# Two mixtures of five paths on VectorE and GpSimd, without identity products on TensorE

## What is computed

```
probs = softmax(logits / tau[:, None], -1)
eps = sigmoid(eps_logit) * 0.2
probs = probs * (1.0 - sum(eps, -1, keepdims=True)) + eps
o = einsum('blhp,blhpd->blhd', probs, paths)          # P = 5 paths
o = o * rsqrt(mean(o * o, -1, keepdims=True) + 1e-05) * norm_w
return o.reshape(b, Ln, D) @ Wo
```

## Time and profile before

| | us |
|---|---|
| median of 3 runs | 425.94 |
| lowest, highest | 425.29, 427.28 |
| the profiled execution | 425.43 |
| its span, first to last instruction | 423.6 |
| TensorE busy (share of the span) | 359.7 (85%) |
| VectorE busy | 308.6 (73%) |
| ScalarE busy | 274.8 (65%) |
| GpSimd busy | 42.0 (10%) |

### The profile page before, as it was taken

One profiled execution on the slowest core, in us unless ns is written; L12 is line 12 of the kernel. 1 busy time (PEld: TensorE's weight loads), 2 busy tenths in 40 slices (PEclk: granted clock), 3 DMA queues, 4 the chain that ended last, 5 costly groups with the idle time before them and its releaser, 6 DMA issues.

```text
span 423.6 us, 9739 instructions
## 1 busy us (share of the span) xinstructions
PE 359.7 (85%) x4096; PEld 267.9 (63%) x4096; DVE 308.6 (73%) x487; ACT 274.8 (65%) x431; POOL 42.0 (10%) x103
## 2 busy tenths in 40 slices
PE   5599999999999898899588379566599994969996
PEld 3387786677866675798576365433267763558885
DVE  2896578737649988999576967867858899597433
ACT  4789875879779787394332354516668843687873
POOL 5000000000000110002888100000000000000000
PEclk9799999999999998889757789685999999889999
DMA  8900005600000000172130000800000000001001
GB/s 279 325 2 1 3 1 183 166 3 2 1 2 0 1 2 3 31 198 66 54 116 3 2 5 2 274 3 2 0 2 2 2 2 1 0 2 46 8 2 50
DMA packets 14469, 19.49 MB, mean 46 GB/s; under 512 B 1104, under 2 KB 9296, under 8 KB 14416
## 3 DMA queue, kind: packets, MB, share of 16 engines
q1 hardware_dynamic: 14128, 18.68, 14.3%
q10 hardware_dynamic: 288, 0.02, 0.1%
HBM read 17.65 MB, written 1.05 MB: 44 GB/s over the span
## 4 chain that ended last, share of the span: by engine, by line
PE 72%; DVE 16%; issue 6%; ACT 4%; DMA 1%; SPq 0%; DVEq 0%; ACTq 0%
PE ps_a L757 14%; PE ps_a L758 13%; PE ps_a L925 6%; PE ps_a L880 4%; PE ps_d L757 3%; PE ps_d L758 3%; PE ps_a L947 3%; PE ps_a L937 2%; PE ps_a L970 2%; PE ps_d L804 2%; PE ps_a L901 2%; PE ps_a L968 2%; PE ps_d L947 2%; PE ps_d L911 2%; PE ps_a L977 2%
## 5 line engine op out<-in xcount | busy, mean ns | idle before, releaser
L757 PE MATMUL ps_a<-acts,w_f 128*128 128x512 f32 x256 | 102.3, 399 | 3.0 <-ACT acts L627 2.1
L758 PE MATMUL ps_a<-acts,w_f 128*128 128x512 f32 x256 | 99.8, 390 | 0.0
L757 PEld LDWEIGHTS ps_a<-acts,w_f 128*128 128x128 f32 x256 | 48.1, 188 | 17.1 <-ACT acts L627 3.7
L758 PEld LDWEIGHTS ps_a<-acts,w_f 128*128 128x128 f32 x256 | 48.1, 188 | 10.3 <-issue 0.7
L627 ACT ACTIVATE acts<-ps_a,vec 128x512 fp32r<-128x512 f32 x64 | 44.5, 696 | 0.0
L1236 DVE TENSOR_TENSOR acts<-ghbuf,acts 128x512 fp32r<-128x512 f32 x32 | 21.2, 689 | 20.8 <-ACT acts L627 20.8
L1236 DVE TENSOR_TENSOR acts<-gbuf,acts 128x512 fp32r<-128x512 f32 x32 | 21.5, 687 | 17.5 <-ACT acts L627 17.4
L624 ACT ACTIVATE gbuf<-ps_a,vec 128x512 f32<-128x512 f32 x32 | 22.2, 695 | 14.1 <-DVE acts L1236 8.4
L880 PE MATMUL ps_a<-xnp,conv_w 128*128 128x512 f32 x108 | 27.3, 407 | 0.0
L624 ACT ACTIVATE ghbuf<-ps_a,vec 128x512 f32<-128x512 f32 x32 | 22.4, 700 | 7.1 <-PE ps_a L758 7.1
L925 PE MATMUL ps_a<-toep,arena 96*32 96x96 f32 x512 | 24.1, 355 | 0.0
(11 more groups left out here) (220 smaller groups left out, 788.5 us busy)
## 6 DMA issues: line engine op xcount, KB each, us to landing
toep<-in_fir SPq DMA_DIRECT2D x24, 288.0 KB, 5.5
w_in<-in_h SPq DMA_DIRECT2D x4, 1024.0 KB, 8.1
g_rows<-in_gW SPq DMA_DIRECT2D x4, 640.0 KB, 5.9
w_in<-in_w SPq DMA_DIRECT2D x6, 256.0 KB, 4.0
iobuf<-in_x SPq DMA_DIRECT2D x4, 256.0 KB, 6.0
y<-iobuf SPq DMA_DIRECT2D x3, 256.0 KB, 2.2
toep<-in_taps SPq DMA_DIRECT2D x1, 512.0 KB, 5.3
toep<-in_proj SPq DMA_DIRECT2D x1, 256.0 KB, 8.3
```

The lines of the kernel that those rows point to most:

```text
L757: e.matmul(bank, w, hi, start=start, stop=False)
L758: return e.matmul(bank, w, lo, start=False, stop=stop)
```

## The change

Each half's mixture is now shared by rows between VectorE and GpSimd. A table `MIX` gives the rows: in half 0 VectorE has rows 0 to 19 and GpSimd 20 to 31, in half 1 each has 16. Both engines start when `probs` rises, multiply their rows by one instruction, and add them by three. `mul`, `add` now have one index per half; the second ones are gone. `addmix` is gone on TensorE and ScalarE. `osq` of VectorE's rows waits for `summed`, that of GpSimd's rows for `pool_sum`; `rms` waits for both squares. In the list, half 0's `add` stands behind recurrence step 1, its first `osq` behind step 2 and its second behind step 3. In `FILL`, half 1's `mul` and `add` keep the places of the first ones before.

```diff
-    s += [("mul", 2, 0), ("first", 2, 1), half[1], ("addmix", 2, 0), ("mul", 2, 1), half[2], ("add", 2, 1), ("osq", 2, 1)]
-    s += [half[3], ("rms", 2, 0), ("round", 2, 0), half[4], ("scale", 2, 0), half[5], ("wo", 2, 0), half[6], ("wo", 2, 1), half[7]]
+    s += [("mul", 2, 0), ("first", 2, 1), half[1], ("add", 2, 0), half[2], ("osq", 2, 0), half[3], ("osq", 2, 1)]
+    s += [("rms", 2, 0), ("round", 2, 0), half[4], ("scale", 2, 0), half[5], ("wo", 2, 0), half[6], ("wo", 2, 1), half[7]]
...
+MIX = ((slice(0, 20), slice(20, 32)), (slice(0, 16), slice(16, 32)))
...
-        ("hid1", 0, 2): [("mul", 2)], ("hid1", 0, 3): [("mul", 3)], ("hid1", 1, 0): [("add", 2)],
-        ("hid1", 1, 3): [("add", 3)], ("hid2", 0, 0): [("osq", 2), ("rms", 1), ("scale", 1)], ("hid2", 0, 1): [("osq", 3)],
+        ("hid1", 0, 2): [("mul", 1)], ("hid1", 1, 0): [("add", 1)],
+        ("hid1", 1, 3): [("osq", 2)], ("hid2", 0, 0): [("osq", 3), ("rms", 1), ("scale", 1)],
...
+        def weights(g, r):
+
+            n = r.stop - r.start
+            return pr5[:, g, r].rearrange("p t c -> p c t").unsqueeze(3).to_broadcast([128, P, n, DH])
...
+            for g in range(G):
+                r = MIX[g][1]
+                e.wait_ge(S["probs"], g + 1)
+                own(e.tensor_tensor(pall[:, :, g, r], pall[:, :, g, r], weights(g, r), ALU.mult))
+                own(e.tensor_tensor(pall[:, 0:2, g, r], pall[:, 0:2, g, r], pall[:, 2:4, g, r], ALU.add))
+                own(e.tensor_tensor(paths[0][:, g, r], paths[0][:, g, r], paths[1][:, g, r], ALU.add))
+                e.tensor_tensor(paths[0][:, g, r], paths[0][:, g, r], paths[4][:, g, r], ALU.add
+                                ).then_inc(S["pool_sum"], 1)
...
-                    r = slice(HB * (i % 2), HB * (i % 2) + HB)
-                    e.wait_ge(S["summed"], i if i else 1)
+                    r = MIX[i // 2][i % 2]
+                    e.wait_ge(S["pool_sum" if i % 2 else "summed"], i // 2 + 1)
...
-                elif kind == "addmix":
-                    e.wait_ge(S["pe_a"], a + 1)
-                    src = bank[:, :].rearrange("p (t c) -> p t c", c=DH)
-                    own(e.activation(paths[0][:, i, 0:HB], src, ACT.Copy))
-                    e.activation(o_sq[:, 0:HB], src, ACT.Square).then_inc(S["act_a"], 1)
...
-                elif kind == "addmix":
-                    e.wait_ge(S["mixed"], 1)
-                    bank = take_a(a)[:, :].rearrange("p (t c) -> p t c", c=DH)
-                    for p in range(P):
-                        last = e.matmul(bank, ident[:, :], paths[p][:, i, 0:HB], start=p == 0, stop=p == P - 1)
-                    last.then_inc(S["pe_a"], 1)
...
                 elif kind == "mul":
...
+                    r = MIX[i][0]
+                    own(e.tensor_tensor(pall[:, :, i, r], pall[:, :, i, r], weights(i, r), ALU.mult))
...
-                    if i == 0:
-                        e.wait_ge(S["act_a"], A_AT[("addmix", 2, 0)] + 1)
-                    e.wait_ge(S["act_osq"], (1, 3)[i])
+                    e.wait_ge(S["act_osq"], 2 * i + 2)
```

More of the change, by code:

```diff
@@ L23 @@
 LN_EPS, L2_EPS, RMS_EPS = 1e-5, 1e-6, 1e-5
-HB, G = DH // 2, 2
+G = 2
 NRING = 4
@@ L102 @@
 RING_A = {"in": 1, "flag": 1, "gsum": 1, "up": KT, "hid1": KT, "hid2": KT, "out": 1, "qkv": 3, "window": 1, "token": 1, "fir": 1,
-          "yy": 1, "bo": 1, "gate": 2, "logit": 1, "addmix": 1}
+          "yy": 1, "bo": 1, "gate": 2, "logit": 1}
 RING_D = {"vproj": 1, "mean": 1, "var": 1, "up": KT, "down": 1, "sumsq": 2, "gram": H, "aq": 1, "rec": 1,
@@ L287, in program @@
                  "act_v act_ss act_nt dve_nrm eye_done l_turned pool_inv inv_done path4 state act_l nums summed act_osq "
-                 "st_zero act_stat dve_stat act_norm path3 st_turned ld_h2 act_exp dve_sub mixed dve_ms act_rms "
-                 "o_turned dve_step act_step pool_step").split()
+                 "st_zero act_stat dve_stat act_norm path3 st_turned ld_h2 act_exp dve_sub dve_ms act_rms "
+                 "o_turned dve_step act_step pool_step probs pool_sum").split()
         S = {n: sem(n) for n in names}
@@ L1090, in late @@
                     settle()
-                    own(e.scalar_tensor_tensor(out=pr5[:, i], in0=pr5[:, i], scalar=vc("rest"),
-                                               in1=vc("eps", 0, P).unsqueeze(1).to_broadcast([128, 32, P]),
-                                               op0=ALU.mult, op1=ALU.add))
-                    settle()
-                elif kind == "mul":
-                    g, r = i // 2, slice(HB * (i % 2), HB * (i % 2) + HB)
-                    w = pr5[:, g, r].rearrange("p t c -> p c t").unsqueeze(3).to_broadcast([128, P, HB, DH])
-                    if i == 0:
[L1099 to L1103, removed]
+                    e.scalar_tensor_tensor(out=pr5[:, i], in0=pr5[:, i], scalar=vc("rest"),
+                                           in1=vc("eps", 0, P).unsqueeze(1).to_broadcast([128, 32, P]),
+                                           op0=ALU.mult, op1=ALU.add).then_inc(S["probs"], 1)
@@ L1104, in late @@
+                    e.wait_ge(S["probs"], i + 1)
+                elif kind == "mul":
+                    r = MIX[i][0]
+                    own(e.tensor_tensor(pall[:, :, i, r], pall[:, :, i, r], weights(i, r), ALU.mult))
+                elif kind == "add":
+                    r = MIX[i][0]
+                    settle()
+                    own(e.tensor_tensor(pall[:, 0:2, i, r], pall[:, 0:2, i, r], pall[:, 2:4, i, r], ALU.add))
                     settle()
-                    own(e.tensor_tensor(pall[:, 0:2, g, r], pall[:, 0:2, g, r], pall[:, 2:4, g, r], ALU.add))
+                    own(e.tensor_tensor(paths[0][:, i, r], paths[0][:, i, r], paths[1][:, i, r], ALU.add))
@@ L1106, in late @@
                     settle()
-                    own(e.tensor_tensor(paths[0][:, g, r], paths[0][:, g, r], paths[1][:, g, r], ALU.add))
-                    settle()
-                    e.tensor_tensor(paths[0][:, g, r], paths[0][:, g, r], paths[4][:, g, r], ALU.add
+                    e.tensor_tensor(paths[0][:, i, r], paths[0][:, i, r], paths[4][:, i, r], ALU.add
                                     ).then_inc(S["summed"], 1)
                 elif kind == "rms":
-                    if i == 0:
-                        e.wait_ge(S["act_a"], A_AT[("addmix", 2, 0)] + 1)
```

## The result

| | before | changed |
|---|---|---|
| median, us (22 runs each) | 425.88 | 428.91 |
| lowest, highest | 422.31, 428.5 | 423.82, 432.38 |
| span of the profiled execution | 423.6 | 427.5 |
| VectorE busy | 308.6 | 313.9 |
| GpSimd busy | 42.0 | 67.9 |

A forecast was written before the change was run, and what follows sets the result against it. VectorE's in-order work, with waits at both mixtures, was taken to bound the kernel. Half 0's +0.2 and half 1's +4.5 made +4.7 us on 425.94, so 430.6 us; likeliest case 428.5 to 432.3, full range 416.5 to 432.3.

The forecast's parts named there:

- The disputed price: Both mixtures: whether VectorE and GpSimd work at the same time when each reads two SBUF operands; +4.7 or -8.4 us.
- strict turns: Both mixtures: VectorE's and GpSimd's two-operand instructions alternate, so their times add; +4.7 us in all, chance 0.58.
- The tiny rows: One-element VectorE instructions: 187 ns beside GpSimd's work against 158 alone, 29 ns longer; weak evidence that the engines alternate.
- rival A: Both mixtures: no effect between the engines, so they overlap freely; -8.4 us, 417.5 us in all, chance 0.30.
- Rival B: Both mixtures: instructions overlap but each is stretched; -1.9 us, 424 us with a spread of 421 to 427, chance 0.12.
- Half 0: First mixture: sum of squares starts at 285.8 against 285.62 us, +0.2; alternation eats the gain from removing the identity products.
- Half 1: Second mixture: VectorE's 9.7 and GpSimd's 9.8 us add, sum of squares at 357.2 against 352.70, +4.5 us.
- Rival C: Second mixture: GpSimd's 4.71 us product precedes the residual at 341.01, delaying the FFN; 431 to 432 us, within the 0.58.
- the mark: Second mixture: start of the sum of squares, at 352.70 us before; the first `wo` product follows it by 7.15 us.
- ScalarE's squares and Gelus: Second mixture: GpSimd's rows' square delays queued Gelus; costed at nothing until GpSimd is later than about 350 us.
- The end of VectorE's adds at 344.9: Second mixture: VectorE's adds end there, its new square precedes a Gelu; 0.6 us on ScalarE, none on the path.
- My term for the clock: First mixture: TensorE at half clock without identity products, 1.08 us per recurrence step, giving back up to 0.9 us.

The follow-up runs named there:

- e5: Changed kernel, but GpSimd only fills its rows with zeros instead of mixing them, so it writes SBUF without reading: 415.31 us, 0.9739 of before.
- e6: Changed kernel, but GpSimd copies its rows onto themselves, reading one SBUF operand, instead of mixing them: 428.5 us, 1.0013 of before.
- e7: Changed kernel, but in half 1 GpSimd starts only behind VectorE's product and the residual after it: 428.08 us, 1.0026 of before.
- e3: Kernel before with only half 1 shared as in the change; half 0 keeps its identity products: 428.32 us, 1.0059 of before.
- e8: Changed kernel plus the ten identity products on TensorE at their old place, as work nobody needs: 427.69 us, 1.0053 of before.
- e1: Kernel before, but half 0 wholly on VectorE, one product for 32 rows, without identity products or GpSimd: 427.35 us, 1.0024 of before.
- e2: Kernel before with only half 0 shared as in the change; half 1 as before: 427.91 us, 1.0044 of before.
- e4: Kernel before, but half 0 on VectorE alone without identity products, two products and split adds ordered to leave no gap: 424.44 us, 0.9963 of before.

## Why the prediction was right, and where it was off

The forecast was 430.6 us, +4.7, with 0.54 on slower; measured was 428.91, +3.0. The likeliest case is the one that happened. The size is in part luck: the two mixtures cost 2.0 us less than forecast, and two stages that had no term in the sum moved by +1.6 and -1.5 us and nearly cancel.

**The disputed price.** Right, and shown: strict turns, by the changed kernel's own ends of instructions and by e5 and e6. The tiny rows leaned the right way, but 29 ns were too little to carry the choice; at 0.58 it was a bet that came out. Without the exclusion the same VectorE work with the same waits gives 0.974 of before (e5; its fills are shorter than GpSimd's products, so this is rival A with a little more than A's gain). Rival B (partial overlap) has no support: apart from the fixed part below, nothing overlaps.

**Half 0, +0.2 us forecast, -0.8 measured.** The order of turns was as written, one by one, and each turn was shorter: 3.37 us for GpSimd's product (forecast 3.58), 1.36 and 1.66 for the first adds (1.49, 1.80), 0.67 and 0.85 for the next (0.82, 1.00), 0.69 for VectorE's last (0.82). What is mis-sized is the fixed part of an instruction. By these differences (an estimate), an instruction that waits for the other engine has already started, and some 0.13 us of its 0.16 to 0.20 are behind it when its turn comes. The six add up to 0.9 us, which is the whole miss.

**Half 1, +4.5 forecast, +3.4 measured.** Sum of times, forecast 9.7 + 9.8 = 19.5, measured 18.50. VectorE's 9.7 are given, which leaves 8.8 for GpSimd against 9.8. The same term: the start of a waiting instruction is hidden, on both engines, and so are the three gaps of 0.08 us between GpSimd's instructions. The price per element from rows of up to 256 elements held for 2560: GpSimd's product, free from the residual's end at 340.36 to 344.89, took 4.5 us of the forecast 4.7, and the hidden start is most of the rest. Rival C, the turn that GpSimd takes ahead of TensorE's next residual, did occur (7.51 us of idle TensorE), but cost at most 0.4 us on the way to the mark, as e7 shows. ScalarE's squares and Gelus, costed at nothing, cost nothing: TensorE had caught up with the hidden layers and waited 1.03 us for VectorE before `wo`. The end of VectorE's adds at 344.9, named there, belongs to the case without turns; they ended at 355.67.

**What was not in the sum.** Two stages moved in which I had costed nothing. Stage D is 69.4 or 69.5 us in the four kernels that share half 1 as the change does (changed, e3, e7, e8), against 70.9 to 72.2 in the four that leave half 1 as it was (before, e1, e2, e4); with GpSimd's work replaced it is 69.3 (e5) and 70.9 (e6). I had noted TensorE's idle 3.86 us before `wo` only as room; but behind it, TensorE's clock was low. The four products of `wo` and eight of the FFN follow there. Their stretch, up to the product behind them, in the order before, changed:

```profile
359.85 3.40 PE L813 MATMUL ps_d<-arena,wo_w 128*128 128x512 f32 x4 [3.86 <-DVE arena L1137]
...
365.21 1.88 PE L804 MATMUL ps_d<-x_t,cent_w 128*128 128x512 f32 x4
```

```profile
365.35 1.98 PE L823 MATMUL ps_d<-arena,wo_w 128*128 128x512 f32 x4 [1.03 <-DVE arena L1135]
...
369.02 1.88 PE L814 MATMUL ps_d<-x_t,cent_w 128*128 128x512 f32 x4
```

The same twelve products take 5.36 us before and 3.67 in the changed kernel, 1.7 us less. The windows over them (before, changed) have the granted clock at 0.57 and at 1.00:

```profile
360.00:364.00 4.00, 4.00 (x7) 1.98 (x8) 2.91 (x6) 2.42 (x4) 0.00 (x0) 0.57 0.00 0
```

```profile
366.00:370.00 4.00, 4.00 (x15) 2.46 (x14) 4.00 (x8) 2.34 (x4) 0.00 (x0) 1.00 0.00 0
```

The stretch is 3.66 to 3.68 us in e3, e5, e7 and e8 too, where TensorE had idled 0.45 to 1.16 us before `wo`, and 5.37 or 5.38 in e1, e2 and e4, where it had idled 3.87 or 3.88; e6, with 2.01 of idle time, has 5.28. So of half 1's +3.4 us at the mark only 1.9 reach the end. That the shorter idle time is what kept the clock up is argued from these rows, not shown by an experiment of its own.

Stage D has a second such place. In the four microseconds that start 24 us behind the mark the granted clock is 0.92 before and 0.94 in the changed kernel, but 0.53 or 0.54 in e1, e2 and e4, whose stage D is 1.2 to 1.3 us longer than before. These three have half 1 as before and no identity products. That is the larger of e2's two losses, and half of what e4 gained in stage A. What sets it stays open, and with one profiled execution of each kernel it is not shown that the level belongs to the kernel and not to the execution; the timed runs of the three agree with it.

Stage B is 53.0 to 53.7 us in the five kernels in which half 0 is shared and GpSimd reads (changed, e2, e6, e7, e8), and 51.7 to 52.4 in the five others. Part of it stands in the clock of two stretches, in the order before, changed:

```profile
295.00:300.00 5.00, 5.00 (x42) 1.84 (x41) 4.24 (x6) 1.90 (x3) 0.00 (x0) 0.96 0.00 0
304.00:310.00 6.00, 4.90 (x11) 2.90 (x12) 5.11 (x8) 4.86 (x8) 0.00 (x0) 0.72 0.00 0
```

```profile
295.00:300.00 5.00, 5.00 (x39) 2.02 (x40) 3.59 (x5) 0.87 (x2) 0.00 (x0) 0.77 0.02 3
304.00:310.00 6.00, 3.84 (x7) 2.43 (x8) 4.95 (x7) 4.39 (x8) 0.00 (x0) 0.51 0.00 0
```

The clock rises later, behind the half's `wo` products, and is lower at the gate's. My term for the clock (up to 0.9 us, in the recurrence steps alone) was in place for stage A, where the clock stayed at 0.50 from 272 to 294 us; stage B had no term, and e8 shows that the missing identity products are not the cause of its loss. What sets it stays open; that five kernels stand on one side and five on the other speaks for a cause in the kernels. e2 shows what it does: stages B and D eat more than stage A's gain.

## What to carry to other kernels

Before work is moved from VectorE to an idle GpSimd, count the SBUF operands of what VectorE does at that time. Where both read tensors in that way (two SBUF operands on VectorE, a read on GpSimd), the times add, and GpSimd's share costs its own longer time: 4.5 us for a product that VectorE does in 2.8. In these traces GpSimd was free help only beside turns, reductions and sums with a PSUM operand, or when it only wrote. An engine's idle gap before a serial step can be filled by order instead: the identity products of half 0 bought nothing that a second VectorE product at their place (e4) didn't buy for less.

## What the runs showed of the hardware that I had not expected

- A waiting instruction's fixed part is paid while it waits: turns of 0.67 us for a 640-element add whose duration alone is 0.82.
- The turn goes to the engine that is already waiting, even when the other has its next instruction queued right behind the one that just ended (GpSimd's product got in when the residual ended at 340.36, ahead of VectorE's product).
- A copy with a single operand on GpSimd excludes VectorE just as a product with two does: two residuals took 5.52 us beside the copies of e6, 4.51 beside the adds of the changed kernel and 1.29 beside fills.
- Work that is late can shorten what follows: TensorE idled 1.03 us before `wo` instead of 3.86, its granted clock was 1.00 instead of 0.57 behind it, and the same twelve products took 3.67 us instead of 5.36.
